# Loading x in three pieces and reordering the first heads, the staged reads and the gap fillers of an audio block kernel

## The reference

```python
h = tok(x)                                   # cubic interpolation x4, windows of 64, 0.5*(x+1.3)^2 + 0.5*exp(-(x-0.7)^2/2),
                                             # |FFT|, M*sigmoid(M - 0.12 max), soft minimum with 0.9 max
xn = layernorm(h)                            # attention over all windows of a signal, 8 heads of 64 features
q, k, v = xn @ Wq, xn @ Wk, xn @ Wv
h = h + relu((sigmoid(q k^T * 8) v) @ Wo)
x2 = layernorm(h)
h = h + shared_mlp(x2) + sum(top-2 of 4 expert MLPs, weighted by a softmax of the two gates)
```

## Time and profile before

| | |
|---|---|
| median of 3 runs | 169.74 us (169.63 to 171.81) |
| the profiled execution | 169.56 us, of which the span from first to last instruction is 167.7 us |
| PE | 150.6 us busy, 90% |
| ACT | 114.9 us busy, 69% |
| DVE | 107.4 us busy, 64% |
| POOL | 53.5 us busy, 32% |
| mean granted TensorE clock | 0.969 of full speed |

### The profile page before, as it was taken

One profiled execution on the slowest core, in us unless ns is written; L12 is line 12 of the kernel. 1 busy time (PEld: TensorE's weight loads), 2 busy tenths in 40 slices (PEclk: granted clock), 3 DMA queues, 4 the chain that ended last, 5 costly groups with the idle time before them and its releaser, 6 DMA issues.

```text
span 167.7 us, 6718 instructions
## 1 busy us (share of the span) xinstructions
PE 150.6 (90%) x2856; PEld 90.8 (54%) x2856; DVE 107.4 (64%) x275; ACT 114.9 (69%) x157; POOL 53.5 (32%) x97
## 2 busy tenths in 40 slices
PE   7599493995996999999999999999999999999890
PEld 2259441443463657575756555544575565765580
DVE  1155898998675695867673848867359883443521
ACT  3388992996766897989987898737727637457420
POOL 3250006956651558182607153426200000000000
PEclk9879569999999999999999999999999999999999
DMA  5920000028567475948566700000000101001002
GB/s 129 199 103 4 0 0 0 0 89 216 132 185 228 122 223 148 262 115 203 138 179 179 189 18 4 0 4 4 0 21 16 34 5 31 24 11 30 21 16 57
DMA packets 14701, 14.00 MB, mean 83 GB/s; under 512 B 1288, under 2 KB 14444, under 8 KB 14608
## 3 DMA queue, kind: packets, MB, share of 16 engines
q1 hardware_dynamic: 14384, 13.42, 30.2%
q10 hardware_dynamic: 288, 0.16, 0.4%
HBM read 8.97 MB, written 4.60 MB: 81 GB/s over the span
## 4 chain that ended last, share of the span: by engine, by line
PE 65%; DVE 10%; DMA 9%; ACT 8%; issue 3%; SPq 2%; DVEq 0%
PE ps L420 12%; PE ps L440 12%; PE ps L541 8%; PE ps L559 7%; PE ps L598 6%; DMA YS<-y_stage 4%; PE ps L451 4%; ACT probs L1134 3%; DMA area<-x_in 3%; PE ps L568 3%; PE ps L297 3%; PE ps L583 2%; PE ps L312 2%; DMA y_stage<-YP 2%; SPq L262 2%
## 5 line engine op out<-in xcount | busy, mean ns | idle before, releaser
L1134 ACT ACTIVATE probs<-ps 125x1000 f32<-125x1000 f32 x64 | 61.8, 1009 | 11.0 <-PE ps L420 10.1
L440 PE MATMUL ps<-probs,xn 124*32 124x250 f32 (+1 forms) x512 | 39.3, 375 | 0.1
L420 PE MATMUL ps<-YS,XT 128*32 128x500 f16 x448 | 34.3, 376 | 3.5 <-DMA YS<-y_stage 3.4
L440 PEld LDWEIGHTS ps<-probs,xn 124*32 124x32 f32 (+1 forms) x512 | 15.9, 109 | 12.3 <-issue 2.5
L1166 ACT ACTIVATE H2r<-ps,wf 128x500 f32<-128x500 f32 x16 | 10.8, 677 | 15.4 <-PE ps L559 15.4
L802 DVE COPY ZS<-ps 128x250 f32<-128x250 f32 x32 | 12.9, 413 | 11.0 <-PE ps L440 10.9
L420 PEld LDWEIGHTS ps<-YS,XT 128*32 128x32 f16 x448 | 10.8, 96 | 11.8 <-DMA YS<-y_stage 4.3
L559 PE MATMUL ps<-area,wf 128*64 128x500 f32 x64 | 16.7, 585 | 0.0
L1004 DVE TENSOR_TENSOR area<-H2r,ps 128x500 f32<-128x500 f32 x16 | 10.8, 674 | 9.2 <-ACT H2r L1166 8.6
L1153 ACT ACTIVATE area<-ps,wf 128x500 f32<-128x500 f32 x24 | 15.9, 672 | 0.9 <-PE ps L541 0.9
L598 PE MATMUL ps<-wf,area 128*61 128x64 f32 (+1 forms) x384 | 14.0, 225 | 0.0
(11 more groups left out here) (151 smaller groups left out, 248.9 us busy)
## 6 DMA issues: line engine op xcount, KB each, us to landing
YS<-y_stage SPq DMA_DIRECT2D x56, 125.0 KB, 3.0
y_stage<-YP SPq DMA_DIRECT2D x14, 250.0 KB, 3.2
tower_out<-res SPq DMA_DIRECT2D x8, 124.0 KB
wf<-wf_in SPq DMA_DIRECT2D x1, 648.0 KB, 7.1
wa<-wa_in SPq DMA_DIRECT2D x1, 512.0 KB, 6.6
area<-x_in SPq DMA_DIRECT2D x1, 210.9 KB
ch<-ch_in SPq DMA_DIRECT2D x1, 160.0 KB, 6.1
tower_out<-res SPq DMA_DIRECT2D x8, 0.5 KB
```

Of the source, the lines that this page charges most:

```text
L420: last = mm(ps[k0:k1, 2 * (n % 2) + j, 0:TG].rearrange("p (h n) -> p h n", h=2), XT[:, g % 3, (2 * bb + cj) * P + k0:(2 * bb + cj) * P + k ...
L440: last = mm(ps[R * hh:R * hh + R, 4 + bb, half * TB:(half + 1) * TB], xn[0:keys, 4 * g + 2 * bb + cj, :], probs[0:keys, n % 3, hh, :], sta ...
L1134: fn(probs[:, n % 3].rearrange("p (j h) n -> p j (h n)", j=2), ps[0:P, 2 * (n % 2):2 * (n % 2) + 2, 0:TG], ACT.Sigmoid, scale=SCORE_SCALE) ...
```

## The change

It has these parts.

1. x comes in three loads (columns of `q = 0`, of `q = 1`, of `q = 2, 3`). The second waits for DVE's memset alone, which now covers its 500 columns, the third for POOL's too, which covers 1000. PE's `q = 2` waits for the third. SP waits until the third is in before it issues the loads of `wa`, `ch` and `wf`.
2. The second half of the distance step is cut: `near` (rows 8 to 19) stays where `others` was, `far` (rows 20 to 31) moves behind the weights' low part on DVE and behind the weights' high part on ACT, ahead of the Sigmoid that loads ACT's table. The variance of `first` loses an instruction (the epsilon goes into the sum before, the factor 8 into later products).
3. Group 0: `y_part` 4 moves from ahead of `scores(0)` to behind it, with `y_part` 5 and both `y_project(1, k)`, ahead of `scores(1)`. Part 4 goes to bank 4, which `mix(0)` writes, so `mix(0)` waits for `yd_lo` 5 in the place of 3. ACT's and DVE's lists are reordered to match; the square of `third` moves from DVE to POOL, and POOL prepares groups 2 and 3 before it splits the feed-forward weights.
4. Fillers in groups 1 to 5 come one or more units earlier. For g >= 2: `x_transpose(g+2)` at t = 0 (was 1), `y_project(g+2, 0)` at t = 1 (was 2), `y_project(g+2, 1)` at t = 3 (was 4), `attn_out(g-1)` at t = 2 (was 3), `x2_transpose(g-2)` at t = 6 (was 7). For g = 1: t = 1, 2, 3 for the three of group 3 (were 3, 4, 5), `attn_out(0)` at 5 (was 4). On DVE `x_take(3)` and `y_take(3, 1)` move up, and `x2_take` goes ahead of `z_take(g, 2)`.
5. SP: from g = 4 on `read_back(g-1, 1)` is issued between `send(g, 0)` and `send(g, 1)`.
6. In the last group of the feed-forward part `layer3(6)` moves ahead of `spread(7, 1)`.

```diff
+TAP_COLS = (slice(0, 4 * P), slice(4 * P, 8 * P), slice(8 * P, NB * P))
...
+        near, far = slice(8, 20), slice(20, 2 * NB)
...
-            for i, cols in enumerate((slice(0, 4 * P), slice(4 * P, NB * P))):
+            for i, cols in enumerate(TAP_COLS):
                 if i:
                     sp.wait_ge(pad_set, 1)
+                if i == 2:
                     sp.wait_ge(pad_pool, 1)
                 sp.dma_start(tapsT[0:TAPS, cols], x[:, cols]).then_inc(taps_in[i], 16)
+            sp.wait_ge(taps_in[2], 16)
             sp.dma_start(wa[:], wa_in).then_inc(attn_w_in, 16)
             sp.dma_start(ch[:], ch_in).then_inc(const16_in, 16)
             sp.dma_start(wf[:], wf_in).then_inc(ffn_w_in, 16)
...
             for g in range(1, NG):
-                for k in range(2):
-                    send(g, k)
-                for k in range(2):
-                    read_back(g, k)
+                send(g, 0)
+                if g >= 4:
+                    read_back(g - 1, 1)
+                send(g, 1)
+                read_back(g, 0)
+                if g <= 2:
+                    read_back(g, 1)
+            read_back(NG - 1, 1)
...
-                if q < 2:
+                if q < 3:
...
-                    pe.wait_ge(yd_lo, 5)
...
-                if i == 5:
-                    pe.wait_ge(yd_lo, 4)
+                if i >= 4:
+                    pe.wait_ge(yd_lo, i - 1)
...
-                if n == 0:
-                    pe.wait_ge(yd_lo, 3)
-                if n == 2:
-                    pe.wait_ge(yd_lo, 6)
+                if n in (0, 2):
+                    pe.wait_ge(yd_lo, 5 + n // 2)
...
-            for i in range(5):
+            for i in range(4):
...
                 if n == 0:
-                    y_part(5)
-                if n == 1:
-                    y_project(1, 0)
-                    y_project(1, 1)
+                    for i in (4, 5):
+                        y_part(i)
+                    for k in range(2):
+                        y_project(1, k)
                 if n == 6:
                     x_transpose(2)
                 if n in (7, 8):
                     y_project(2, n - 7)
 
-                if t == (3 if g == 1 else 1) and 1 <= g < NG - 2:
+                if t == (1 if g == 1 else 0) and 1 <= g < NG - 2:
                     x_transpose(g + 2)
-                if t == (4 if g == 1 else 2) and 1 <= g < NG - 2:
+                if t == (2 if g == 1 else 1) and 1 <= g < NG - 2:
                     y_project(g + 2, 0)
-                if t == (5 if g == 1 else 4) and 1 <= g < NG - 2:
+                if t == 3 and 1 <= g < NG - 2:
                     y_project(g + 2, 1)
 
-                if t == (4 if g == 1 else 3) and g >= 1:
+                if t == (5 if g == 1 else 2) and g >= 1:
                     if g + 2 < NG:
                         pe.wait_ge(xt_cp, g + 3)
                     else:
                         pe.wait_ge(x2t_cp, g - 2)
                     attn_out(g - 1)
-                if t == 7 and g >= 2:
+                if t == 6 and g >= 2:
                     x2_transpose(g - 2)
...
+                if g == NG - 1:
+                    layer3(g - 1)
...
-                if 1 <= g <= NG:
+                if 1 <= g <= NG and g != NG - 1:
                     layer3(g - 1)
...
-            v.memset(tapsT[:, 4 * P:10 * P], 0.0).then_inc(pad_set, 1)
+            v.memset(tapsT[:, 4 * P:8 * P], 0.0).then_inc(pad_set, 1)
...
+            masked_size(first)
             distance(first)
             dve.wait_ge(act1, 4)
-            distance(others)
+            masked_size(others)
+            distance(near)
...
-            total(first, masked)
-            variance(first)
+            total(first, masked, F * EPS)
+            dve1_at["squares", first.start] = st.n
             dve.wait_ge(wprod_hi, 1)
             low = scoreW[F:128].rearrange("p (i s) r f -> p i (s r f)", i=2)
             v.scalar_tensor_tensor(low, ps[F:128, 6:8, 0:4 * F], QSCALE, low,
                                    ALU.mult, ALU.subtract).then_inc(wprod_lo, 1)
-            dve.wait_ge(act1, 6)
-            soft_minimum(third)
+            distance(far)
 
...
+            dve.wait_ge(act1, 6)
+            soft_minimum(third)
             x_take(0)
             total(third, tok)
-            for i in range(4):
+            for i in range(2):
+                part_low(i)
+            centre(third)
+            for i in range(2, 4):
                 part_low(i)
             x_take(1)
-            part_low(4)
-            centre(third)
-            part_low(5)
-            square(third)
             y_take(1, 0)
+            dve.wait_ge(square_pool, 1)
             total(third, masked)
             variance(third)
+            part_low(4)
             y_take(1, 1)
+            part_low(5)
 
             z_take(0, 0)
+            dve.wait_ge(act1, 7)
             soft_minimum(later)
...
             z_take(0, 3)
             y_take(2, 1)
+            x_take(3)
             z_take(1, 0)
-            x_take(3)
             y_take(3, 0)
+            y_take(3, 1)
             z_take(1, 1)
-            y_take(3, 1)
             z_take(1, 2)
...
+                x2_take(g - 2)
                 z_take(g, 2)
-                x2_take(g - 2)
                 squares2(g - 1)
...
-            distance_plus(others)
+            distance_plus(near)
             act.wait_ge(vfold_mm, 1)
             fn(wvT[:].rearrange("p h n -> p (h n)"), ps[0:F, 3, 0:H * R], ACT.Copy).then_inc(wv_cp, 1)
             act.wait_ge(wprod_mm, 1)
             fn(scoreW[:].rearrange("p (i s) r f -> p i (s r f)", i=2), ps[:, 6:8, 0:4 * F],
                ACT.Copy, scale=QSCALE).then_inc(wprod_hi, 1)
+            distance_plus(far)
             act.wait_ge(idle_set, 1)
...
-            for i in range(5):
+            for i in range(4):
                 part_high(i)
...
-                if n == 0:
-                    part_high(5)
                 if n in (1, 2):
-                    second_high(n - 1)
+                    part_high(n + 3)
+                if n in (0, 1):
+                    second_high(n)
                 if n == 6:
...
-            v.memset(tapsT[:, 10 * P:NB * P], 0.0).then_inc(pad_pool, 1)
+            v.memset(tapsT[:, 8 * P:NB * P], 0.0).then_inc(pad_pool, 1)
...
-            inverse_deviation(slice(0, 4), first)
-            inverse_deviation(slice(4, 8), first)
+            pool.wait_ge(dve1, dve1_at["squares", first.start])
+            for g in range(2):
+                rows = slice(4 * g, 4 * g + 4)
+                v.tensor_tensor(norm[:, 4, rows], norm[:, 2, rows], half_neg[0:P, rows], ALU.pow).then_inc(rstd_done, 1)
+            pool.wait_ge(rstd_done, 2)
+            v.tensor_scalar(norm[:, 4, 4:8], norm[:, 4, 4:8], float(F) ** 0.5, None, ALU.mult).then_inc(rstd_done, 1)
             split_rows(1)
             pool.wait_ge(wprod_lo, 1)
             for k in range(2):
                 v.tensor_copy(scoreP[:, k].rearrange("p (j i) r -> p i j r", i=2),
                               scoreW[:, :, 0, :].rearrange("p (i a j) r -> p i a j r", i=2, a=2)[:, :, k]).then_inc(packed, 1)
-
+            pool.wait_ge(dve1, dve1_at["centred", third.start])
+            v.tensor_tensor(masked[:, third, :], mag[:, third, 0:NBIN], mag[:, third, 0:NBIN],
+                            ALU.mult).then_inc(square_pool, 1)
+            inverse_deviation(slice(8, 12), third)
+            split_rows(2)
+            inverse_deviation(slice(12, 16), third)
...
-            inverse_deviation(slice(8, 12), third)
-            split_rows(2)
-            inverse_deviation(slice(12, 16), third)
-            split_rows(3)
-            inverse_deviation(later, later)
+            inverse_deviation(slice(16, 20), later)
+            split_rows(4)
+            inverse_deviation(slice(20, 32), later)
...
-                if g + 3 < NG:
+                if 5 <= g + 3 < NG:
```

26 lines of the change are left out of this document (17 added, 9 removed).

## The result

The changed kernel takes 179.75 us (median of 4 runs, 177.57 to 180.53) against 169.99 (4 runs of the kernel before beside them, 169.63 to 171.81): ratio 1.051, interval [1.037, 1.064]. It is slower, as forecast, but by 9.8 us and not by 4; the time lies above the range. The profiled execution took 177.57 us, span 175.8, against 169.56 and 167.7.

The account below looks back on a forecast made before the run. PE, without idle time in mid-attention, was taken as the bound, with time to win at the start and two data waits. Terms -2.6 + 0 + 0.15 + 2.1 + 4.3 + 0.2 = +4.15 on 169.56 gave 173.7 us, range 169.0 to 175.6.

Parts of the forecast that it names:

- E: Groups 2 to 5: the earlier `y_project(g+2, 0)` waits for DVE's copy of XT, 1.07 us in each group; +4.3 us.
- B: Norms up to group 0's products: 0.5 us gained on DVE is lost behind ACT's late table load; zero.
- F: Tail, last feed-forward group: `layer3(6)` fills a 0.43 us wait but is longer than it; +0.2 us.
- A: The start: with x in three loads the last square can start at about 12.0, 2.6 us earlier.
- third rival: The start gives less (-1.0) because the third load or `wa` lands late: 175.3 us; chance 0.15 together with the fourth rival.
- C: Group 0: PE stands ahead of `mix(0)` for `part_low(4)`, then steps cost 0.57 + 0.57; +0.15 us to `scores(8)`.
- fourth rival: PE's long waits put 2 us of its work at the lower clock: 175.7 us; chance 0.15 together with the third rival.
- D: Group 1: PE waits at `x_transpose(3)` (2.1 us) and `y_project(3, 1)` (1.95) for DVE's copies; +2.1 us.

Follow-up runs that it names:

- xt_first: The changed kernel with DVE's copy of XT for group g+2 moved ahead of the copy `z_take(g-1, 3)`; ratio to the kernel before 1.022.
- early_alone: The kernel before with only the fillers of groups 2 to 7 a step earlier (and `x2_take`); ratio to the kernel before 1.024.
- outw_first: The changed kernel with ACT's copy of `outW` ahead of the Softplus of `far` and the table load; ratio to the kernel before 1.055.
- g0_warm: The kernel before with group 0's new order and five unneeded matmuls filling the wait ahead of `mix(0)`; ratio to the kernel before 1.003.
- g0_alone: The kernel before with only the change's new order of group 0; ratio to the kernel before 1.018.
- loads_xt: The kernel before with x in three loads, early fillers, and the copy of XT ahead of `z_take(g-1, 3)`; ratio to the kernel before 0.992.
- three_loads: The kernel before with only x in three loads and the weights issued once x is in; ratio to the kernel before 0.995.
- loads_nowait: The kernel before with x in three loads and the weights issued at once behind them, without waiting for x; ratio 0.989.

## Why the prediction was wrong, point by point

**The direction, E and B were right.** E was forecast at +4.3 and measured +3.96; four waits of the projection for DVE's copy of XT, 1.06 us each in issue time. xt_first and early_alone show both halves of the mechanism. B was forecast at 0 and is +0.05: the first `y_part` waits 1.13 us for `outW`, which comes at 27.85 out of the late table load, and outw_first frees 0.60. F was +0.2 and is +0.19. Groups 6 and 7, for which nothing was forecast, take 0.36 longer (19.22 against 18.86). It is the wait of `mix(62)` for its sigmoid (0.62 us), which comes with the early `x2_transpose(5)`. The forecast said that this filler costs nothing, because what it waits for is done; what it had covered was left out.

**A: the step that failed is "then ACT sets the pace".** Its times of x were right (third load in by 5.1), and its result of about 12.0 is what xt_first shows. But ACT's 1.24 us a quarter sets the pace only if TensorE's two passes are shorter, and in the prediction's own rows they were not: six passes in 4.48 us are 1.49 a quarter, most of them at a granted clock of 0.50. An estimate from these rows laid end to end has the last pass done at 3.65 + 1.10 + 4.48 = 9.23. The last square came 3.68 behind that point before (14.66 against 10.98), so it would start at about 12.9, which is 1.75 earlier and not 2.6. The rest is that the length in one execution was taken for the length. The first pair took 1.10 us there and 2.03 in g0_warm, with the same start. The clock of this stretch differs between executions, and the interpolation is what is exposed once x is early: 3.83 us with fast passes, 7.13 with slow ones. The bounds (1.5 to 2.9) held no term for it. The third rival gave the size (-1.0), for a wrong reason: neither the third load nor `wa` was late. The sentence on issuing `wa` early, by which the later issue gives 0.4 us back, was not borne out: with or without the wait, nobody waited for `wa`.

**C: the step that failed is the one behind the wait, "from there steps of `scores` and `mix` cost 0.57 + 0.57".** The wait is right: 1.7 forecast, 1.96 measured, for `part_low(4)`. Of the steps behind it three took 1.0 us and one 0.77, 1.5 us more in all. This is the fourth rival, and it was sized well (2 us) but given too small a chance, and as an accident beside the forecast. It belonged inside C, since C itself made the wait. The argument against it was that 1.89 and 1.47 us ahead of groups 1 and 2 did not bring the clock down. That was one execution, and those waits stand in another place. For group 1 the argument even held in seven executions of eight, with waits of up to 2.74 us; ahead of `mix(0)` it failed in seven of seven. What makes the difference is open. It isn't that TensorE has more to do behind the waits of group 1: in g0_warm it is busy for 6.46 of the 6.46 us behind `mix(0)` too (36.14 to 42.60). The Trainium skill ("TensorE: Matmul & The Clock Gate", "HAM oscillation — how this bites in real kernels") says that waits between bursts of matmuls let the clock fall, which costs again behind each of them. The prediction wrote that the trace did not agree. In group 0 the runs agree (8.00 us in g0_alone against 6.53 in g0_warm behind the same wait, empty or filled), though the wait is shorter than those of the page's example; in group 1 seven of eight executions do not.

**D: the mechanism was right and one term mis-sized.** The second wait is 1.93 for 1.95. The first is 2.74 for 2.1 (of which the sum counted 1.7), because the sum took only DVE's `z_take` and `y_take` as queued ahead and not the last norm's sums (1.1 us), whose cover was the data wait that the same step let vanish. 2.74 + 1.93 less the old 1.47 and the 0.22 of the earlier trace rows is 2.98; measured +3.02.

The misses add up: +1.65 (A), +1.32 (C), +0.92 (D), -0.34 (E), +0.40 elsewhere make 3.95, the distance from the forecast sum of +4.15 to +8.1. The median lies another 2.2 us above the profiled execution, where before it lies 0.4 above (169.99 against 169.56). The four runs of this kernel spread by 3.0 us, the four of before by 2.2, and the traces at hand do not say where the slowest of these runs lost it.

## What to carry to other kernels

An instruction that is pulled ahead on one engine has to be followed into the lists of the engines that feed it: here a projection moved one step forward met a copy that was queued behind one which waits for the matmuls just ahead of it, and exchanging two lines on DVE gave all 4 us of these waits back. When a stage loses a wait, list what other engines did under it, for that work is now behind the next instruction of the chain. The same holds for a filler that leaves its place: ask what wait it covered there. And a new wait on TensorE is priced with the steps behind it at both levels of the clock, from rows of more than one execution; where it can't be removed, filling it with matmuls for nobody is worth a try.

## What the runs showed of the hardware that was not expected

- In group 0 an empty wait of 1.9 us was followed, after none to two steps at full speed, by a stretch at the lower clock (granted 0.51 from 35.70 to 39.20 in the changed kernel), in seven executions out of seven; with 1.24 us of needless matmuls in the wait, in none of two. In group 1 waits of 2.2 to 2.7 and of 1.9 us brought it in one execution out of eight.
- A stretch at a granted clock of 0.50 ahead of that wait (30.60 to 33.90 in g0_alone) came and went from one execution to the next, also with the order of the kernel before (early_alone and loads_xt have it, three_loads and loads_nowait do not). What sets it is open.
- The same start gave an interpolation of 3.83 us or 7.13 us for the same eight passes, behind the same six warm-up matmuls. What sets this is open. The Trainium skill ("TensorE: Matmul & The Clock Gate", "What's actually happening") says that the number of slow matmuls at a kernel's start changes from run to run; these traces agree.
- `wa` took 4.8 us from issue to landing when issued behind x (5.03), 5.6 when issued at 2.23, and 6.6 in the kernel before, all of it hidden.
